# Scores of an attention kernel in four column tiles of 32 keys, with side pieces moved ahead of the branches

## The chip, the cores and the metric

The kernel runs on one core of a Trainium2 chip. The metric is the device time of one execution in microseconds (us); a measurement of this kernel tells changes of about 0.3% from no change.

## The reference, cut to what matters

Four blocks follow one another on x of shape (4, 2048, 256), each on the layernorm of x and added to x: attention A, a feed-forward block, attention B, the feed-forward block again. All weights are 256 x 256, and each attention has 16 heads of 16 channels.

```python
# attention A                                     # attention B
q, k, v = heads(xn @ Wq.T), ...                   k = decayed sums of heads(xn @ Wk.T), normed, scaled
scores = q @ k.T * 0.25, causal                   v = mix of v and v one later, normed, scaled
out = softmax(scores) @ v @ Wo.T                  y1 = softmax(k[1:] @ k.T, causal) @ v; out = y1 @ Wc.T
# feed-forward
x_prev = x one token earlier;  xr, xk = mixes of x and x_prev
out = sigmoid(xr @ Wr.T) * ((relu(xk @ Wk.T) ** 2) @ Wv.T)
```

## The kernel before, in words

**Instances and slots.** There are eight attentions (four batches, A and B), in the order of ATT (L48). Each is worked through in four instances of four heads (HG), so n runs from 0 to 31. head_group() (L52) cuts an instance into 68 groups: for each chunk of 512 queries (qc) and each block of 128 keys (kb) up to the diagonal, two groups of two heads, and at the diagonal narrower ones (512, 384, 256 and 128 queries wide). A group fills two PSUM banks with scores, keys on the 128 partitions and queries along the bank. The time of the program is written out by hand in slots, one slot per group: in slot s TensorE computes the scores of group s + 3 (scores, L998), then the products of the values with the probabilities of group s, where a set is due (products, L1034), and then the side pieces. ScalarE takes the exponential of one group, 128 x 1024 (L810), into probs. GpSimd zeroes the upper triangle in groups on the diagonal (L713), five of them per chunk.

**Scores.** One matmul (L1013) has 99 rows (the channels of q and k as split into bf16 parts, and three rows for a maximum), 128 keys as its weights and up to 512 queries as its moving operand, in bf16. It uses all 128 columns of the array. **Products.** One set is four matmuls in fp32, one per head (L1055), each with 17 weight columns written to PSUM partitions 32 j to 32 j + 16: four column tiles of 32. The trace counts every fp32 matmul twice, once for each pass, so a set of four shows as x8. Of the 68 slots, 36 have products.

**Side pieces.** Between these run the projections, layernorms and feed-forward blocks of other chunks, as jobs (job_list, L124): P projects a chunk for an attention A, MA finishes a chunk after attention A and prepares it for attention B, MB finishes it after attention B. Tables T_P, T_M and T_B (L112 to L118) give each piece a slot behind the job's t0. o0 and o1 (project_tokens, L870, matmul L875) are the output projection, t0, t1, bt0 and bt1 are transposes (turn, L857, matmul L860) that wait for the layernorm of VectorE (L1121 to L1130), u0 to u3 are projections of keys and queries (project_channels, L863, matmul L866). Side pieces use the whole array. P has 10 pieces with TensorE, MB 10 and MA 18. A job that belongs to an instance has its t0 three slots ahead of that instance's first slot, those of attention A of batch 1 have it 8 slots behind.

**Branches.** Where a head's scores could be too large for an exponential without a maximum, a flag is set. TensorE reads a flag per instance (L1083) and branches (L1084): into a body that first computes the maxima (maxima, L982; row_maxima, L962) and then 68 slots with a mask matmul (L1017) on the diagonal, or past it into the else part, 68 slots without. The branch of instance n stands in front of slot 68 n - 3. The two bodies lie behind each other in the instruction stream, so an instance without a flag jumps over the first body, and one with a flag jumps over the second when it is done. With these inputs four instances have a flagged head, one head each: n = 11, 15, 27 and 31, the last of each attention B. maxima() first waits for all the loads of keys and queries of the instance, which SyncE issues (load_keys, load_queries), then for each head reads a flag and branches again (L991).

**Order.** Each engine walks the slots in order. VectorE, ScalarE and GpSimd issue the jobs' steps in slots of the same tables. Score groups have three buffers (NS_BUF), so the scores of group g wait for the exponential of group g - 3, and probs has six.

Of the kernel before, what the change touches and what calls it, by code (L numbers as in the profile page):

```python
# [12 lines left out]
P = 128  # L13
# [4 lines left out]
CH = 512  # L18
NCH = S // CH
# [61 lines left out]
AHEAD = NS_BUF  # L81

FIRST_OF = [min(i for i, g in enumerate(GROUPS) if g[0][0][0] == qc) for qc in range(NCH)]
LAST_OF = [max(i for i, g in enumerate(GROUPS) if g[0][0][0] == qc) for qc in range(NCH)]
# [39 lines left out]
def job_list():  # L124
    def start(k, c):
        return (k * NHG + c) * NG

    jobs = [Job("P", 0, c, 0, -80 + 14 * c) for c in range(NCH)]
    for c in range(NCH):
        jobs.append(Job("P", 1, c, 1, start(0, c) + 8))  # L130
    for k, b in ((1, 0), (2, 1), (5, 2), (6, 3)):
        jobs += [Job("MA", b, c, k + 1, start(k, c) - 3) for c in range(NCH)]
    for k, b in ((3, 0), (4, 1)):
        for c in range(NCH):
            jobs.append(Job("MB", b, c, k, start(k, c) - 3))
            jobs.append(Job("P", b + 2, c, k + 1, start(k, c) + 29))
    jobs += [Job("MB", 2, c, 7, start(7, c) - 3 if c < 3 else start(7, 2) + 32) for c in range(NCH)]

    jobs += [Job("MB", 3, c, 7, start(7, 3) + (16, 37, 58, 82)[c]) for c in range(NCH)]
    jobs.sort(key=lambda j: j.t0)  # L140
    return jobs


JOBS = job_list()
FIRST_SLOT = -100
W_FIRST = (WQ, WK, WV)
# [96 lines left out]
def hybrid_kernel(nc, t, out):  # L243
    with ExitStack() as ctx:
# [571 lines left out]
        def _(pe):  # L816
# [27 lines left out]
            def setup(slot):  # L844
# [3 lines left out]
                if slot == JOBS[3].t0:  # L848
                    params()

            def free_bank(part):
                if part.before:
# [109 lines left out]
            def row_maxima(n, j):  # L962
                i0 = (n * HG + j) * NMP
                kk, qq = k_st[0:KROWS, j, :], q_st[0:KROWS, j, :]
                for i, (qb, b0, nb) in enumerate(MAX_PIECES):
                    if i >= MAX_BUF:
                        pe.wait_ge(s_mx["used"], i0 + i + 1 - MAX_BUF)
# [14 lines left out]
            def maxima(n):  # L982
                if n:
                    pe.wait_ge(s_probs, n * NG)
                for c in range(NCH):
                    pe.wait_ge(s_q[c], 16 * (len(Q_RUNS) + 1) * (n + 1))
                    pe.wait_ge(s_k[c], 16 * len(K_RUNS) * (n + 1))
                k, hg = divmod(n, NHG)
# [9 lines left out]
            def scores(g, masked):  # L998
# [10 lines left out]
                for bank, units in enumerate(GROUPS[i]):  # L1009
                    o = ps[:, 2 * (g % NS_BUF) + bank, :]  # L1010
                    for qc, kb, j, q0, w, col in units:
                        mask = masked and kb >= TB * qc
                        last = pe.matmul(o[:, col:col + w], k_st[0:KROWS, j, kb * P:(kb + 1) * P],  # L1013
                                         q_st[0:KROWS, j, qc * CH + q0:qc * CH + q0 + w], start=True, stop=not mask,
                                         skip_group_check=mask)
                        if mask:
                            last = pe.matmul(o[:, col:col + P], mask_qk[:, :], ident_b[:, :], start=False, stop=True,  # L1017
                                             skip_group_check=True)
                last.then_inc(s_scores, 1)
# [55 lines left out]
            for n in range(NI):  # L1075
# [7 lines left out]
                any_flag = pe.value_load(flags_of(k)[:, H + hg:H + hg + 1])  # L1083
                with pe.If(any_flag > 0):  # L1084
                    maxima(n)
                    slots(n * NG - AHEAD, (n + 1) * NG - AHEAD, True)
                with pe.Else():
                    pe.sem_inc(s_mx["scores"], NMP * HG)
                    pe.sem_inc(s_mx["turned"], HG)
                    slots(n * NG - AHEAD, (n + 1) * NG - AHEAD, False)  # L1090
            slots(NTOT - AHEAD, LAST_SLOT, False)

# [351 lines left out]
```

## Time and profile before

| | us |
|---|---|
| median of three runs | 3423.64 (3422.43 to 3432.76) |
| profiled execution, its own time | 3428.78 |
| span of the profiled execution | 3427.0 |
| mean granted clock of TensorE, share of full | 0.957 |
| busy: TensorE / ScalarE / VectorE / GpSimd | 3151.7 / 2291.9 / 1423.6 / 850.3 |

A row of the timeline view has the start in us, the us from start to end of what it merges, the engine, the line, the operation, out<-in, shapes and a count; in brackets stands the idle time before it and what ended it. A matmul's recorded length holds a tail of about 0.16 us in which the next one already runs, so the distance of two starts is the time that a matmul takes from the next. PEld is the weight load. "issue" means that the profile shows nothing that was waited for.

### The profile page before, as it was taken

To read this page: it belongs to the slowest core of one execution; us is meant where nothing else is said; L and a number is where in the kernel's file an instruction comes from. 1 tells how busy PE (TensorE), PEld (TensorE's weight loads), DVE (VectorE), ACT (ScalarE), POOL (GpSimd) and SP (SyncE) were. 2 spreads that over 40 slices of the span, in tenths; PEclk is the share of its full clock that TensorE was granted. 3 is DMA by queue.
4 is the path that set the end of the run, shared out by engine and by line. 5 is a ranking of instruction groups with operands and counts; after the bars stand their busy time and mean duration, and the time that the engine had idled before them with its cause. 6 is when DMAs were issued, how large, how long until landed. Compare 5 with 4: busy or idle time off the path is not lost.

```text
span 3427.0 us, 51952 instructions
## 1 busy us (share of the span) xinstructions
PE 3151.7 (92%) x19172; PEld 1212.5 (35%) x19172; DVE 1423.6 (42%) x3534; ACT 2291.9 (67%) x2487; POOL 850.3 (25%) x1278
## 2 busy tenths in 40 slices
PE   7999999999999789997999999999999989899897
PEld 4222233333333333332333333333333333333334
DVE  5222235545454542434233333445445545422434
ACT  2788767777676467674667676776777764688462
POOL 4111123333222222221222221323233221322111
PEclk9999999999999899998999999999999998999899
DMA  5222212222221123222212222121222211222111
GB/s 139 78 74 67 83 43 68 68 66 67 57 65 48 53 59 85 63 59 62 79 55 71 74 79 86 54 59 52 69 64 67 71 52 37 62 63 75 41 44 44
DMA packets 229682, 223.05 MB, mean 65 GB/s; under 512 B 33221, under 2 KB 212933, under 8 KB 229320
## 3 DMA queue, kind: packets, MB, share of 16 engines
q1 hardware_dynamic: 228504, 217.47, 22.2%
q8 instruction: 223, 3.65, 0.5%
q14 instruction: 139, 1.14, 0.1%
q10 hardware_dynamic: 816, 0.79, 0.1%
HBM read 146.80 MB, written 71.32 MB: 64 GB/s over the span
## 4 chain that ended last, share of the span: by engine, by line
PE 77%; DVE 10%; issue 7%; ACT 4%; POOL 1%; SPq 1%; DMA 1%; ACTq 0%; DVEq 0%; POOLq 0%
PE ps L1055 26%; PE ps L1013 25%; PE ps L875 12%; PE ps L866 10%; ACT probs L810 4%; DVE pmax L1349 2%; PE ps L860 2%; DVE ln_st L1121 1%; DVE xn L1130 1%; DVE o_blk L1391 1%; POOL v_st L691 1%; DVE x_buf L1242 1%; PE ps L903 0%; DVE nw_u L1111 0%; DVE nw_u L1113 0%
## 5 line engine op out<-in xcount | busy, mean ns | idle before, releaser
L810 ACT ACTIVATE probs<-ps 128x1024 f32<-128x1024 f32 x2176 | 2136.5, 1023 | 749.8 <-PE ps L1013 555.8
L1013 PE MATMUL ps<-q_st,k_st 99*128 99x512 bf16 (+3 forms) x5120 | 1204.3, 353 | 120.6 <-issue 103.5
L1055 PE MATMUL ps<-probs,v_st 128*17 128x512 f32 (+3 forms) x10240 | 1163.1, 535 | 41.9 <-ACT probs L810 16.2
L713 POOL TENSOR_SCALAR_AFFINE_SELECT probs<-probs 128x256 f32<-128x256 f32 (+1 forms) x896 | 423.4, 487 | 1705.9 <-ACT probs L810 1700.4
L1013 PEld LDWEIGHTS ps<-q_st,k_st 99*128 99x128 bf16 x5120 | 424.0, 98 | 1062.4 <-ACT probs L810 467.8
L1055 PEld LDWEIGHTS ps<-probs,v_st 128*17 128x17 f32 x10240 | 185.0, 96 | 534.5 <-issue 355.6
L1391 DVE STREAM_TRANSPOSE o_blk<-ps 128x512 f32<-128x512 f32 x128 | 90.8, 710 | 449.4 <-PE ps L1055 449.4
L866 PE MATMUL ps<-xT,wT 128*128 128x512 f32 x512 | 255.6, 625 | 1.6 <-issue 1.0
L1242 DVE TENSOR_TENSOR x_buf<-x_buf,ps 128x512 f32<-128x512 f32 x64 | 43.4, 679 | 380.1 <-PE ps L875 380.1
L637 POOL TENSOR_TENSOR parts<-rest,parts 128x512 bf16<-128x512 f32 x96 | 119.9, 1249 | 260.8 <-DVE parts L1153 260.8
L1266 DVE SCALAR_TENSOR_TENSOR buf_v<-buf_v,ps 128x512 f32<-128x512 f32 x64 | 44.0, 687 | 304.8 <-PE ps L875 304.8
L875 PE MATMUL ps<-wT,o_in 128*128 128x256 f32 x512 | 160.4, 468 | 1.0 <-issue 1.0
L662 POOL TENSOR_TENSOR buf_a<-xf 128x512 f32<-128x512 f32 x64 | 79.4, 1242 | 270.7 <-DVE xf L1136 255.2
L866 PEld LDWEIGHTS ps<-xT,wT 128*128 128x128 f32 x512 | 90.7, 193 | 140.9 <-issue 128.8
L866 PE MATMUL ps<-buf_k,wT 128*128 128x512 f32 x256 | 125.8, 616 | 8.3 <-DVE buf_k L1253 8.3
L875 PEld LDWEIGHTS ps<-wT,o_in 128*128 128x128 f32 x512 | 117.7, 236 | 41.5 <-issue 20.0
L875 PE MATMUL ps<-wT,buf_a 128*128 128x256 f32 x512 | 126.6, 391 | 0.5 <-issue 0.5
L875 PE MATMUL ps<-wT,buf_u 128*128 128x256 f32 x512 | 121.2, 380 | 2.2 <-issue 2.2
L760 ACT CAST parts<-ps 128x512 bf16<-128x512 f32 x64 | 37.4, 585 | 114.0 <-PE ps L866 114.0
L860 PE MATMUL ps<-ident,xn 128*128 128x128 f32 x512 | 83.7, 288 | 29.9 <-DVE xn L1130 14.5
L875 PEld LDWEIGHTS ps<-wT,buf_a 128*128 128x128 f32 x512 | 92.5, 190 | 48.7 <-issue 38.4
L972 PE MATMUL ps<-k_st,q_st 99*128 99x512 bf16 (+3 forms) x160 | 65.5, 525 | 45.9 <-issue 38.3
(136 smaller groups left out, 2152.0 us busy)
## 6 DMA issues: line engine op xcount, KB each, us to landing
part_a<-parts SPq DMA_DIRECT2D x192, 128.0 KB
x_buf<-in_L_attn_a_X SPq DMA_DIRECT2D x32, 512.0 KB, 4.5
q_st<-part_a SPq DMA_DIRECT2D x128, 128.0 KB
o_chan<-o_out SPq DMA_DIRECT2D x64, 256.0 KB, 2.4
o_in<-o_chan SPq DMA_DIRECT2D x64, 256.0 KB, 4.5
q_st<-part_b SPq DMA_DIRECT2D x128, 128.0 KB
k_st<-part_a SPq DMA_DIRECT2D x64, 192.0 KB, 2.9
part_b<-parts SPq DMA_DIRECT2D x96, 128.0 KB
```

The costliest lines, as they stand in the source:

```text
L637: pool.tensor_tensor(parts[:, u % NPARTS, 2, :], rest[:, u % 2, :], parts[:, u % NPARTS, 1, :], ALU.subtract).then_inc(s_low, 1)
L662: pool.tensor_tensor(buf_a[:, kt, :], xf[:, kt, 1:CH + 1], xf[:, kt, 0:CH], ALU.subtract).then_inc(s_diff, 1)
L713: last = pool.affine_select(out=o, in_=o, compare_op=ALU.is_ge, fill=0.0, base=0, pattern=[[0, o.shape[1]], [1, P]], channel_multiplier=-1)
L810: nc.scalar.activation(probs[:, g % NP_BUF, :], ps[:, bk:bk + 2, :].rearrange("p a n -> p (a n)"), ACT.Exp, scale=SCALE[ATT[g // (NHG * NG ...
L860: last = pe.transpose(ps[:, part.bank, tb * P:(tb + 1) * P], src[:, tb, kt * P:(kt + 1) * P], ident[:, :])
L866: last = pe.matmul(ps[:, part.bank, :], wT[:, w, kt, m * P:(m + 1) * P], src[:, kt, :], start=(kt == 0), stop=(kt == KT - 1))
L875: last = pe.matmul(ps[:, part.bank, i * D:(i + 1) * D], src[:, kt, tb * P:(tb + 1) * P], wT[:, w, kt, :], start=(kt == 0), stop=(kt == KT ...
L1013: last = pe.matmul(o[:, col:col + w], k_st[0:KROWS, j, kb * P:(kb + 1) * P], q_st[0:KROWS, j, qc * CH + q0:qc * CH + q0 + w], start=True, ...
L1055: last = pe.matmul(ps[32 * j:32 * j + VW, bank, q0:q0 + w], v_st[:, k % 2, kb, hg * HG + j, :], p, start=(kb == 0), stop=(kb >= TB * qc), ...
L1242: nc.vector.tensor_tensor(half(x, i), half(x, i), ps[:, part.bank, :], ALU.add).then_inc(s_side[part.bank], 1)
L1349: nc.vector.tensor_reduce(pmax[:, 1 if b0 else 0, qb:qb + 1], src, AX_X, ALU.max).then_inc(s_mx["used"], 1)
L1391: nc.vector.transpose(o_blk[:, sg % 2, :], ps[:, 6 + sg % 2, :]).then_inc(s_o, 1)
```

## The change

Every matmul of scores(), the one on keys and queries and the one that adds the mask, is issued as four, one for each 32 keys, each to 32 PSUM partitions, with the same moving operand. The jobs of an instance start one slot earlier (FRONT is -4), so that their first piece, o0, is issued in the last slot ahead of the branch; the P jobs of batch 1 start 27 slots earlier, so that u2 falls there; the lead-in starts 10 slots earlier. The branch tests for a flag of 0, and the body without maxima comes first. maxima() no longer waits for all loads; row_maxima waits for a chunk's loads ahead of the first block of queries of that chunk.

```diff
--- before.py
+++ after.py
@@ -80,6 +80,8 @@
 NP_BUF = 6
 AHEAD = NS_BUF
 
+FRONT = -AHEAD - 1
+
 FIRST_OF = [min(i for i, g in enumerate(GROUPS) if g[0][0][0] == qc) for qc in range(NCH)]
 LAST_OF = [max(i for i, g in enumerate(GROUPS) if g[0][0][0] == qc) for qc in range(NCH)]
 DIAG_OF = [min(i for i, g in enumerate(GROUPS) if g[0][0][0] == qc and g[0][0][1] == TB * qc) for qc in range(NCH)]
@@ -125,16 +127,16 @@
     def start(k, c):
         return (k * NHG + c) * NG
 
-    jobs = [Job("P", 0, c, 0, -80 + 14 * c) for c in range(NCH)]
+    jobs = [Job("P", 0, c, 0, -90 + 14 * c) for c in range(NCH)]
     for c in range(NCH):
-        jobs.append(Job("P", 1, c, 1, start(0, c) + 8))
+        jobs.append(Job("P", 1, c, 1, start(0, c) + FRONT - T_P["u2"]))
     for k, b in ((1, 0), (2, 1), (5, 2), (6, 3)):
-        jobs += [Job("MA", b, c, k + 1, start(k, c) - 3) for c in range(NCH)]
+        jobs += [Job("MA", b, c, k + 1, start(k, c) + FRONT) for c in range(NCH)]
     for k, b in ((3, 0), (4, 1)):
         for c in range(NCH):
-            jobs.append(Job("MB", b, c, k, start(k, c) - 3))
+            jobs.append(Job("MB", b, c, k, start(k, c) + FRONT))
             jobs.append(Job("P", b + 2, c, k + 1, start(k, c) + 29))
-    jobs += [Job("MB", 2, c, 7, start(7, c) - 3 if c < 3 else start(7, 2) + 32) for c in range(NCH)]
+    jobs += [Job("MB", 2, c, 7, start(7, c) + FRONT if c < 3 else start(7, 2) + 32) for c in range(NCH)]
 
     jobs += [Job("MB", 3, c, 7, start(7, 3) + (16, 37, 58, 82)[c]) for c in range(NCH)]
     jobs.sort(key=lambda j: j.t0)
@@ -142,7 +144,7 @@
 
 
 JOBS = job_list()
-FIRST_SLOT = -100
+FIRST_SLOT = -110
 W_FIRST = (WQ, WK, WV)
 W_LATER = (FR, FK, FV, BK, BV, WO, BC)
 LAST_SLOT = NTOT + 140
@@ -848,6 +850,12 @@
                 if slot == JOBS[3].t0:
                     params()
 
+            def matmul(o, kt, q, **how):
+
+                for c in range(0, P, 32):
+                    last = pe.matmul(o[c:c + 32], kt[:, c:c + 32], q, **how)
+                return last
+
             def free_bank(part):
                 if part.before:
                     pe.wait_ge(s_side[part.bank], part.before)
@@ -963,6 +971,9 @@
                 i0 = (n * HG + j) * NMP
                 kk, qq = k_st[0:KROWS, j, :], q_st[0:KROWS, j, :]
                 for i, (qb, b0, nb) in enumerate(MAX_PIECES):
+                    if qb % TB == 0:
+                        pe.wait_ge(s_q[qb // TB], 16 * (len(Q_RUNS) + 1) * (n + 1))
+                        pe.wait_ge(s_k[qb // TB], 16 * len(K_RUNS) * (n + 1))
                     if i >= MAX_BUF:
                         pe.wait_ge(s_mx["used"], i0 + i + 1 - MAX_BUF)
                     for bk in range(b0, b0 + nb):
@@ -982,9 +993,6 @@
             def maxima(n):
                 if n:
                     pe.wait_ge(s_probs, n * NG)
-                for c in range(NCH):
-                    pe.wait_ge(s_q[c], 16 * (len(Q_RUNS) + 1) * (n + 1))
-                    pe.wait_ge(s_k[c], 16 * len(K_RUNS) * (n + 1))
                 k, hg = divmod(n, NHG)
                 for j in range(HG):
                     flag = pe.value_load(flags_of(k)[:, hg * HG + j:hg * HG + j + 1])
@@ -1010,12 +1018,12 @@
                     o = ps[:, 2 * (g % NS_BUF) + bank, :]
                     for qc, kb, j, q0, w, col in units:
                         mask = masked and kb >= TB * qc
-                        last = pe.matmul(o[:, col:col + w], k_st[0:KROWS, j, kb * P:(kb + 1) * P],
-                                         q_st[0:KROWS, j, qc * CH + q0:qc * CH + q0 + w], start=True, stop=not mask,
-                                         skip_group_check=mask)
+                        last = matmul(o[:, col:col + w], k_st[0:KROWS, j, kb * P:(kb + 1) * P],
+                                      q_st[0:KROWS, j, qc * CH + q0:qc * CH + q0 + w], start=True, stop=not mask,
+                                      skip_group_check=mask)
                         if mask:
-                            last = pe.matmul(o[:, col:col + P], mask_qk[:, :], ident_b[:, :], start=False, stop=True,
-                                             skip_group_check=True)
+                            last = matmul(o[:, col:col + P], mask_qk[:, :], ident_b[:, :], start=False, stop=True,
+                                          skip_group_check=True)
                 last.then_inc(s_scores, 1)
 
             def values_there(n, qc):
@@ -1081,13 +1089,13 @@
                     for bk in SIDE_BANKS[:2]:
                         pe.wait_ge(s_side[bk], parts_before(bk, 0))
                 any_flag = pe.value_load(flags_of(k)[:, H + hg:H + hg + 1])
-                with pe.If(any_flag > 0):
-                    maxima(n)
-                    slots(n * NG - AHEAD, (n + 1) * NG - AHEAD, True)
-                with pe.Else():
+                with pe.If(any_flag == 0):
                     pe.sem_inc(s_mx["scores"], NMP * HG)
                     pe.sem_inc(s_mx["turned"], HG)
                     slots(n * NG - AHEAD, (n + 1) * NG - AHEAD, False)
+                with pe.Else():
+                    maxima(n)
+                    slots(n * NG - AHEAD, (n + 1) * NG - AHEAD, True)
             slots(NTOT - AHEAD, LAST_SLOT, False)
 
         @block.vector
```

## Rows read from the trace of the kernel before

**Rows 1.** The page: span, and busy time of each engine with its share.

```profile
span 3427.0 us, 51952 instructions
...
PE 3151.7 (92%) x19172; PEld 1212.5 (35%) x19172; DVE 1423.6 (42%) x3534; ACT 2291.9 (67%) x2487; POOL 850.3 (25%) x1278
```

**Rows 2.** The page's costliest groups: scores, and two sorts of token projections.

```profile
L1013 PE MATMUL ps<-q_st,k_st 99*128 99x512 bf16 (+3 forms) x5120 | 1204.3, 353 | 120.6 <-issue 103.5
...
L875 PE MATMUL ps<-wT,o_in 128*128 128x256 f32 x512 | 160.4, 468 | 1.0 <-issue 1.0
...
L875 PE MATMUL ps<-wT,buf_u 128*128 128x256 f32 x512 | 121.2, 380 | 2.2 <-issue 2.2
```

**Rows 3.** Timeline of TensorE, 578 to 589 us, within an instance.

```profile
578.56 0.61 PE L1013 MATMUL ps<-q_st,k_st 99*128 99x512 bf16 x2
579.00 1.89 PE L875 MATMUL ps<-wT,buf_u 128*128 128x256 f32 x8
580.73 0.60 PE L1013 MATMUL ps<-q_st,k_st 99*128 99x512 bf16 x2
581.26 1.05 PE L1055 MATMUL ps<-probs,v_st 128*17 128x512 f32 x8
...
583.21 1.05 PE L1055 MATMUL ps<-probs,v_st 128*17 128x512 f32 x8
...
588.10 0.66 PE L860 MATMUL ps<-ident,xn 128*128 128x128 f32 x4
```

**Rows 4.** Timeline of TensorE, 531 to 543 us, around a branch without a flag.

```profile
531.20 1.05 PE L1055 MATMUL ps<-probs,v_st 128*17 128x512 f32 x8 [1.41 <-POOL probs L713]
535.77 1.01 PE L1013 MATMUL ps<-q_st,k_st 99*128 99x512 bf16 x2 [3.52 <-issue]
536.58 3.48 PE L875 MATMUL ps<-wT,o_in 128*128 128x256 f32 x8
...
541.96 0.63 PE L1055 MATMUL ps<-probs,v_st 128*17 128x256 f32 x8
542.52 2.00 PE L875 MATMUL ps<-wT,o_in 128*128 128x256 f32 x8
```

**Rows 5.** Line 1084, the branch in TensorE's sequencer: min/median/max in ns.

```profile
L1084 PEldq COMPARE_BRANCH  x36: 82/3690/4694, 90.8 to 3371.7; - x36
```

**Rows 6.** Waits of TensorE: us in total, times, longest us.

```profile
PE ps L1013 <- issue: 103.5, 28, 7.7
...
PE ps L1055 <- POOL probs L713: 11.7, 14, 1.4
```

**Rows 7.** Window 533 to 540 us: busy per engine; PEclk is the granted clock.

```profile
533.00:540.00 7.00, 4.23 (x11) 3.04 (x12) 0.32 (x1) 1.02 (x1) 3.81 (x6) 0.51 0.42 111
```

**Rows 8.** Timeline of TensorE: first matmul of flagged instance 11, first after it.

```profile
1135.24 0.28 PE L972 MATMUL ps<-k_st,q_st 99*128 99x128 bf16 x1 [9.91 <-issue]
...
1266.36 1.01 PE L1013 MATMUL ps<-q_st,k_st 99*128 99x512 bf16 x2 [7.73 <-issue]
```

**Rows 9.** Groups by shape: scores 128 queries wide.

```profile
L1013 PE MATMUL ps<-q_st,k_st 99*128 99x128 bf16 x512 | 112.5, 220 | 0.0
```

**Rows 10.** Timeline of TensorE in a flagged instance: narrow scores and their mask.

```profile
1254.92 0.22 PE L1013 MATMUL ps<-q_st,k_st 99*128 99x128 bf16 x1
1254.98 0.22 PE L1017 MATMUL ps<-ident_b,mask_qk 128*128 128x128 bf16 x1
```

**Rows 11.** Timeline after the last branch: a run of narrow products, and its weight loads.

```profile
3375.55 1.49 PE L1055 MATMUL ps<-probs,v_st 128*17 128x384 f32 x24 [1.90 <-issue]
...
3376.21 0.34 PEld L1055 LDWEIGHTS ps<-probs,v_st 128*17 128x17 f32 x12 [0.20 <-issue]
```

**Rows 12.** Timeline of VectorE, 582 to 589 us: the last step of a layernorm.

```profile
586.63 1.38 DVE L1130 TENSOR_SCALAR xn<-x_buf,ln_mv,nw_y 128x256 f32<-128x256 f32 x4
```

**Rows 13.** Timeline of TensorE: first scores of the program.

```profile
94.99 4.43 PE L1013 MATMUL ps<-q_st,k_st 99*128 99x512 bf16 x16 [5.88 <-issue]
```

**Rows 14.** Timeline of ScalarE, 1002 to 1006 us: two exponentials in a row.

```profile
1004.36 1.94 ACT L810 ACTIVATE probs<-ps 128x1024 f32<-128x1024 f32 x2 [0.44 <-PE ps L1013]
```

## The prediction, made before the changed kernel ran

> **What bounds the kernel now.** I read the page's head first: TensorE is busy for 92% of the span and ScalarE for 67% [rows 1], so time is saved where TensorE stands between matmuls, or runs slowly. The costliest groups come next: 5,120 score matmuls [rows 2], 160 for each of 32 instances. Then the timeline inside an instance [rows 3]. Two scores behind side work take 0.44 us up to the next side piece (578.56 to 579.00), so 0.22 each. The same two take 0.53 up to the values' products (580.73 to 581.26). So going from the whole array to column tiles costs 0.09. A set of products 256 wide takes 0.56 up to the next matmul [rows 4]; one 512 wide, up to the scores, 0.98 (583.21 less four scores and 0.09 before it is 582.24, which is 0.98 behind 581.26). The extra 256 columns cost 0.42, so 512 are 0.85 and the way back costs 0.13. A pair of slots takes 1.95 (581.26 to 583.21), of which 0.22 goes into two switches: 0.11 each.
>
> The second loss is at the branches. Behind the products at 531.20 TensorE idles 3.52 us, with nothing waited for [rows 4]; the branch has a median of 3,690 ns [rows 5]. There are 28 such idle times, 103.5 us in all [rows 6]: 24 between two instances without a flag, 3 behind flagged ones (two jumps in a row, 7.73 us [rows 8]) and one at the start. The granted clock is 0.51 over 533 to 540 us, so most of that stretch is at 1.2 GHz, behind the idle time [rows 7]. The piece o0 issued there takes 3.48 us where its like takes 1.89 [rows 3, 4].
>
> **The change, part by part.** The sum is made against the profiled execution's 3,428.8 us, span 3,427.0; the median of 3,423.6 is 5 us below it.
>
> *Scores in tiles.* Now each of 36 product slots in an instance has a switch before it and one behind, 2,298 in all with those at the ends taken off. Afterwards scores and products share a mode, and only side pieces switch. By the tables they occupy 548 slots behind the first, each with a switch in and one out: 1,095. Some of these are new, where a side piece sits in a slot without products. 1,203 switches fewer at 0.11: **-132**. Against it stands the layernorm. xn is ready at 588.01 [rows 12] and the transposes start at 588.10 [rows 3] with no idle time: TensorE arrives just then. The seven slots before it become 0.7 us shorter, and VectorE's chain does not, so the 16 second layernorms of the MA jobs give that back: **+12**. The first layernorm of each job already keeps TensorE waiting, partly for the taking of a segment queued behind it, and t0 moves to a slot ahead of that dependence, so I charge nothing there; if that cover fails it is another +20.
>
> Does a group of four take 0.22 as the one matmul did? The products show four tiles side by side, but in fp32. The trace has no bf16 ones. The densest stretch has 24 matmuls in 1.49 us, and within it 12 weight loads in 0.34, three groups of four about 0.12 apart [rows 11]. So 0.22 for a group is within what the queue has fed, and I take 0 extra. The upper bound is the mean of the same stretch, 0.062 per load and matmul: 0.25 a group, +0.03 x 5,120 = +154. Below, nothing is gained, as the moving operand is as long as before. Scores 128 wide are another matter: today the matmul behind one starts 0.06 later [rows 10], and the densest groups of four are about 0.11 apart. There are 512 [rows 9], so 0 to +26, plus the masks of four instances; I take a middle value of 0.03, **+15**.
> The Trainium skill has a rule against this part: in "TensorEngine Tiling (Array Packing)", Restrictions and Gotchas, column tiling switches Fast Weight Load off. With "TensorE: Matmul & The Clock Gate", LDWEIGHTS, a load takes its columns over 1.2 GHz, 107 ns for four times 32; by this estimate the 512 narrow groups would cost 24 us in place of 15, the wide ones nothing. No run so far shows it for bf16.
>
> *A piece ahead of the branch.* The sequencer passes on o0's eight matmuls before it jumps, so they run in the fetch's shadow. At full clock they take 1.73 (579.00 to 580.73, [rows 3]). 24 boundaries x 1.73: **-42**. u2 in front of the first instances is as long. The idle time left is 3.5 - 1.7 = 1.8 us. o0 and o1 are 160.4 us busy, the equally long L875 group on buf_u 121.2 [rows 2]; of the 39 us between them some 10 belong to the flagged instances, and the scores beside them (1.01 against 0.60 us [rows 3, 4]) add about 5. If 1.8 us of idle time no longer brings the clock down, that is **-34**; bounds 0 and -45.
>
> *The branch turned round.* Between two unflagged instances nothing changes: a taken jump at the entry becomes one at the exit, both at the same place. Behind a flagged one both jumps go, at three places: 7.73 + 1.6 each, **-28**. At the end of instance 31 its exit jump goes as well: 1.90 [rows 11], **-2**. At the start 3.7 us of jump go [rows 5, 13], but TensorE's queue is now passed by P of batch 1, chunk 0: its layernorm (up to 7.1 us, from 580.9 to 588.0 [rows 3, 12]) can start only behind the flags, then come two transposes and u0 to u2. Instance 0 starts some 8 us later and has 6 us less in it: **+2**. VectorE, SyncE (its loads) and GpSimd are passed by the same job, and wait for nothing that isn't there by then. In front of each of the four flagged instances there are now two jumps. Today's 9.91 us of idle time [rows 8] is loads that are still coming, then four inner flags. Two jumps take as long as those loads or longer, less the cover of o0. From -2.6 to +6.8 each; I take 1.5, as the longest jump is 4.7 [rows 5]: **+6**.
>
> *Waits by chunk.* Behind two jumps all loads are there: **0**. Without the jumps it would be worth some part of the 9.91 us at each of four places. Only TensorE's own maxima are queued behind these waits, and VectorE, which takes them.
>
> *One slot earlier.* GpSimd's values for the next attention (L691) now come ahead of the first diagonal mask of the last chunk, not between two. The 11.7 us that products wait for masks [rows 6] go: **-12**, at worst 0. The DMAs of the jobs start a slot earlier on SyncE's queue, ahead of the branch's place, and their data is needed a slot earlier too: 0.
>
> Sum: -132 + 12 + 15 - 42 - 34 - 28 - 2 + 2 + 6 + 0 - 12 = **-215**. 3,428.8 - 215 = 3,213.8, and 5 less for the median: **3,209**.
>
> **The rivals.**
>
> *ScalarE sets the pace.* Two exponentials in a row take 1.94 - 1.02 = 0.92 from start to start [rows 14], 1.84 a pair, while TensorE would do 1.74. Then a pair without side work gains 0.11, not 0.21. For it: in such stretches ScalarE is already nearly always busy. Against it: TensorE gains 0.05 to 0.07 a slot on it and may be some two slots ahead, so it takes about 27 slots without side work to catch up, and every side piece of 1.7 us resets that. If it bound in half the pairs, some 50 us would be lost: 3,259. Chance 0.12.
>
> *The clock still falls.* Idle time of 1.8 us still brings 1.2 GHz, and the fetch under load is longer than the cover. Then the 34 go, and half of the 42 may: 3,209 + 34 + 21 = 3,264, up to 3,290. Chance 0.10.
>
> *The feed of instructions binds.* Scores go from 5,120 loads and matmuls to 20,480. If a pair of them takes 0.062 us, as the mean in rows 11 has it, a group takes 0.25: 3,209 + 154 = 3,363. For it: no longer stretch of the trace is that dense. Against it: 12 loads in 0.34 us in the same stretch, and products between the scores need only half the rate. Chance 0.10.
> The Trainium skill, "TensorE: Matmul & The Clock Gate", says that the sequencer's microcode spends about 62 ns for a MATMUL when hardware decoding is off; four are 0.248 us, which gives about the same time. The 12 loads speak neither for nor against it, since it counts matmuls.
>
> *Slower than before: tiles in bf16 do not run side by side.* The same moving operand is then read four times in turn, wholly or in part. Four in a row would take 0.88 and add 0.66 x 5,120 = 3,380: 6,600 us. With half an overlap, 0.44 a group, +1,126: 4,335. It decides from 215 / 5,120 = 0.042 us on, a group of 0.262. For it: a bf16 operand of 512 columns passes in 0.22 and an fp32 one in twice 0.42, so the rate of columns per tile would be twice what the products have shown. Against it: at two passes and four bytes the products move the same bytes per us and tile. Chance 0.07.
>
> **How the numbers follow.** The forecast has 0.58, the rivals 0.12, 0.10, 0.10 and 0.07, and 0.03 lies between the last two, within 0.3% of before. The median is predicted by the likeliest, 3,209. Its own bounds (masks not gained, narrow scores at +26, the first layernorm at +20 on one side; 34 to 45 for the clock and shorter idle time on the other) give 3,160 to 3,260. With the first two rivals the range is 3,150 to 3,295; what is left out is the feed, the serial tiles and the case between, 0.20. Faster by over 0.3% (about what a measurement can tell): 0.58 + 0.12 + 0.10 + 0.10 = 0.90; within it 0.03; slower 0.07.
>
> **What would show it.** Right: pairs of slots start 1.74 to 1.78 us apart; no 0.11 between scores and products; four score matmuls start within 0.03 of one another and groups 0.22 apart. At the boundaries o0 stands in front of 1 to 2 us of idle time, in windows where the clock stays at full; flagged instances have over 9 us before L972 and none behind them. The layernorm before bt0 shows TensorE waiting for VectorE. Wrong: groups of scores over 0.24 apart would mean feed or port; a pair at 1.84 with ScalarE back to back means ScalarE; a clock of half behind each boundary takes the 34 away; and a new wait for xn at t0 as well would cost up to 20.

## The result, and the profile after

| | before | after |
|---|---|---|
| median | 3427.38 us (3422.43 to 3432.76, 6 runs) | 3447.16 us (3445.12 to 3456.79, 6 runs) |
| span of the profiled execution | 3427.0 | 3443.4 |
| mean granted clock | 0.957 | 0.942 |

The ratio is 1.0062, 95% interval 1.005 to 1.0073: 20 us slower, where 215 us less had been forecast. The forecast was wrong in sign, and its range, 3,150 to 3,295, missed by 152 us. The page's head, beside [rows 1]:

```profile
span 3443.4 us, 84234 instructions
...
PE 3067.8 (89%) x35300; PEld 1346.3 (39%) x35300; DVE 1444.8 (42%) x3534; ACT 2241.7 (65%) x2487; POOL 833.8 (24%) x1278
```

TensorE is busy 84 us less and the span is 16 longer: what the tiles won came back as idle time. In the densest stretch the tiles do what was forecast. TensorE's timeline:

```profile
520.24 1.04 PE L856 MATMUL ps<-q_st,k_st 99*32 99x512 bf16 x16
521.10 1.03 PE L1063 MATMUL ps<-probs,v_st 128*17 128x512 f32 x8
521.96 1.04 PE L856 MATMUL ps<-q_st,k_st 99*32 99x512 bf16 x16
...
637.71 1.05 PE L856 MATMUL ps<-q_st,k_st 99*32 99x384 bf16 x32
638.58 1.03 PE L1063 MATMUL ps<-probs,v_st 128*17 128x512 f32 x8
```

A pair of slots starts 1.72 us behind the last (1.95 before, [rows 3]). Four groups of four score matmuls take 0.86, so 0.215 a group, and the switch to the products is gone. At 637.71 eight groups, two 384 wide, two 128 and four 256, take 0.87 us, no more than their 2,048 columns do at 0.215 for 512: narrow groups cost nothing extra. The waits of TensorE (us in total, times, longest), before, beside [rows 6], and after:

```profile
PE ps L860 <- DVE xn L1130: 14.5, 2, 9.6
...
PE ps L860 <- DVE o_blk L1391: 11.1, 29, 0.6
PE ps L1055 <- issue: 10.1, 26, 1.9
```

```profile
PE ps L1063 <- issue: 63.4, 56, 2.6
PE ps L856 <- issue: 57.9, 29, 3.7
PE ps L868 <- DVE o_blk L1399: 57.8, 29, 2.4
PE ps L868 <- DVE xn L1138: 51.3, 19, 13.8
PE ps L983 <- issue: 50.5, 5, 13.5
PE ps L1063 <- ACT probs L812: 25.3, 17, 2.0
```

A segment is what the products of one chunk of queries sum up in one bank, and VectorE takes it out with the transpose into o_blk. The idle time in front of scores with nothing waited for (L856) has fallen from 103.5 to 57.9, and L983, the first matmul of a flagged instance, has risen from 38.3 to 50.5. Both moved the way that was forecast; the rise of 12 is twice the 6 forecast. New are the transposes t0 (L868), which wait 57.8 us for the taking of a segment where it was 11.1, and 51.3 for xn where it was 14.5, and the products (L1063), where 63.4 was 10.1. By the trace's records of the granted clock, 399 us now run at 1.2 GHz (48 stretches) where it was 294 (36). In instance 6, TensorE before, from o1 to t0, and after:

```profile
640.80 1.99 PE L875 MATMUL ps<-wT,o_in 128*128 128x256 f32 x8
...
650.44 0.63 PE L860 MATMUL ps<-ident,xn 128*128 128x128 f32 x4 [0.34 <-DVE o_blk L1391]
```

```profile
628.10 1.99 PE L883 MATMUL ps<-wT,o_in 128*128 128x256 f32 x8
631.79 1.05 PE L856 MATMUL ps<-q_st,k_st 99*32 99x512 bf16 x16 [1.70 <-issue]
...
634.90 1.99 PE L883 MATMUL ps<-wT,o_in 128*128 128x256 f32 x8
...
637.27 0.61 PE L1063 MATMUL ps<-probs,v_st 128*17 128x256 f32 x8
...
642.07 0.61 PE L856 MATMUL ps<-q_st,k_st 99*32 99x512 bf16 x8
644.83 0.81 PE L868 MATMUL ps<-ident,xn 128*128 128x128 f32 x4 [2.15 <-DVE o_blk L1399]
645.57 1.04 PE L856 MATMUL ps<-q_st,k_st 99*32 99x512 bf16 x8
648.64 1.91 PE L1063 MATMUL ps<-probs,v_st 128*17 128x512 f32 x8 [2.03 <-ACT probs L812]
```

And VectorE after, in the same stretch:

```profile
637.01 0.69 DVE L1250 TENSOR_TENSOR x_buf<-x_buf,ps 128x512 f32<-128x512 f32 x1 [4.33 <-PE ps L883]
637.81 1.41 DVE L1129 BATCH_NORM_STATS2 ln_st<-x_buf 128x6 f32<-128x256 f32 x4
...
642.68 1.38 DVE L1138 TENSOR_SCALAR xn<-x_buf,ln_mv,nw_y 128x256 f32<-128x256 f32 x4
643.98 0.71 DVE L1399 STREAM_TRANSPOSE o_blk<-ps 128x512 f32<-128x512 f32 x1
...
646.31 0.67 DVE L1399 STREAM_TRANSPOSE o_blk<-ps 128x512 f32<-128x512 f32 x1
...
647.86 0.68 DVE L1144 COPY xf<-ps 128x512 f32<-128x512 f32 x1
```

o0 (628.10) does cover the branch: 1.70 us of idle time, at full clock. But o1 (634.90) now stands ahead of the instance's last products (637.27), and VectorE issues the layernorm (637.81 to 644.06) ahead of the taking of those products (643.98). TensorE is at t0 at 642.68 and waits 2.15 us, where instance 6 waited 0.34 before. xn is ready at 644.06; what t0 waits for last is the taking of that last segment (643.98 to 644.69), since t0's bank is the one that it lay in. Then the products at 648.64 wait again. The view names ScalarE, whose probs had long been there; what ended then is VectorE's copy of t0 (647.86 to 648.54). t0 is now in slot 5, and seg_at gives that slot bank 7, which these first products of chunk 1 are to fill. In slot 6, before, it was bank 6. In the instances on either side this second stall is put down to "issue" (2.5 to 2.6 us), which is most of the new 63.4; run e14 below, with t0 in the other bank, has 7.5 there. The window that holds both stalls:

```profile
644.00:653.00 9.00, 6.14 (x44) 2.18 (x48) 4.99 (x13) 2.20 (x4) 1.04 (x1) 0.62 0.42 118
```

TensorE is busy 6.14 of 9 us, and the clock is mostly at the lower level (0.62): 1.2 GHz from 645.1 to 652.0, from just behind the first of the two waits. At the start of the program, in TensorE's, SyncE's and VectorE's timelines:

```profile
102.58 1.97 PE L868 MATMUL ps<-ident,xn 128*128 128x128 f32 x8 [13.79 <-DVE xn L1138]
...
115.42 1.30 PE L856 MATMUL ps<-q_st,k_st 99*32 99x512 bf16 x16 [2.74 <-issue]
```
```profile
84.40 5.59 SPq L435 DMA_DIRECT2D part_a<-parts  x9
90.03 1.11 SPq L421 DMA_DIRECT2D x_buf<-in_L_attn_a_X  x1
```
```profile
96.91 1.41 DVE L1129 BATCH_NORM_STATS2 ln_st<-x_buf 128x6 f32<-128x256 f32 x4 [7.64 <-DMA x_buf<-in_L_attn_a_X]
```

The moved job's load of x stands behind nine stores on SyncE's queue. Its layernorm starts at 96.91, and the first scores come 20.4 us later than before (94.99, [rows 13]).

### The profile page after: what moved, and what is told of

Read it like the earlier page. It is cut to its first block, busy times and chain, and to the rows that moved or that the text cites. A ratio compares the mean times of both kernels' runs of the same rounds, so it can differ in the third digit from the quotient of the medians.

```text
span 3443.4 us, 84234 instructions
## 1 busy us (share of the span) xinstructions
PE 3067.8 (89%) x35300; PEld 1346.3 (39%) x35300; DVE 1444.8 (42%) x3534; ACT 2241.7 (65%) x2487; POOL 833.8 (24%) x1278
## 3 DMA queue, kind: packets, MB, share of 16 engines
q8 instruction: 345, 5.65, 0.7%
## 4 chain that ended last, share of the span: by engine, by line
PE 74%; DVE 13%; issue 7%; ACT 3%; SPq 1%; DMA 1%; POOL 0%; DVEq 0%; ACTq 0%; POOLq 0%
PE ps L856 24%; PE ps L1063 24%; PE ps L883 12%; PE ps L874 11%; ACT probs L812 3%; PE ps L868 3%; DVE pmax L1357 2%; DVE ln_st L1129 2%; DVE xn L1138 2%; DVE nw_u L1119 1%; DVE nw_y L1123 1%; DVE nw_u L1121 1%; DVE x_buf L1250 1%; DVE ln_mv L1132 1%; DVE o_blk L1399 1%
## 5 line engine op out<-in xcount | busy, mean ns | idle before, releaser
L812 ACT ACTIVATE probs<-ps 128x1024 f32<-128x1024 f32 x2176 | 2076.7, 1082 | 787.3 <-PE ps L856 783.5
L856 PE MATMUL ps<-q_st,k_st 99*32 99x512 bf16 (+3 forms) x20480 | 1264.9, 354 | 75.9 <-issue 57.9
L1063 PE MATMUL ps<-probs,v_st 128*17 128x512 f32 (+3 forms) x10240 | 1197.5, 544 | 92.3 <-issue 63.4
L856 PEld LDWEIGHTS ps<-q_st,k_st 99*32 99x32 bf16 x20480 | 496.1, 96 | 965.6 <-issue 584.4
L715 POOL TENSOR_SCALAR_AFFINE_SELECT probs<-probs 128x256 f32<-128x256 f32 (+1 forms) x896 | 408.5, 472 | 1639.4 <-ACT probs L812 1617.9
L1063 PEld LDWEIGHTS ps<-probs,v_st 128*17 128x17 f32 x10240 | 273.8, 99 | 387.8 <-issue 151.4
L868 PE MATMUL ps<-ident,xn 128*128 128x128 f32 x512 | 98.1, 325 | 113.4 <-DVE o_blk L1399 57.8
L868 PEld LDWEIGHTS ps<-ident,xn 128*128 128x128 f32 x512 | 64.8, 162 | 182.0 <-DVE xn L1138 135.0
L883 PE MATMUL ps<-wT,o_in 128*128 128x256 f32 x512 | 131.6, 401 | 0.2 <-issue 0.2
L983 PE MATMUL ps<-k_st,q_st 99*128 99x512 bf16 (+3 forms) x160 | 66.7, 533 | 57.0 <-issue 50.5
L883 PEld LDWEIGHTS ps<-wT,buf_u 128*128 128x128 f32 x512 | 92.3, 189 | 62.0 <-issue 51.8
```

The source lines that it names most:

```text
L715: last = pool.affine_select(out=o, in_=o, compare_op=ALU.is_ge, fill=0.0, base=0, pattern=[[0, o.shape[1]], [1, P]], channel_multiplier=-1)
L812: nc.scalar.activation(probs[:, g % NP_BUF, :], ps[:, bk:bk + 2, :].rearrange("p a n -> p (a n)"), ACT.Exp, scale=SCALE[ATT[g // (NHG * NG ...
L856: last = pe.matmul(o[c:c + 32], kt[:, c:c + 32], q, **how)
L868: last = pe.transpose(ps[:, part.bank, tb * P:(tb + 1) * P], src[:, tb, kt * P:(kt + 1) * P], ident[:, :])
L883: last = pe.matmul(ps[:, part.bank, i * D:(i + 1) * D], src[:, kt, tb * P:(tb + 1) * P], wT[:, w, kt, :], start=(kt == 0), stop=(kt == KT ...
L1063: last = pe.matmul(ps[32 * j:32 * j + VW, bank, q0:q0 + w], v_st[:, k % 2, kb, hg * HG + j, :], p, start=(kb == 0), stop=(kb >= TB * qc), ...
```

## The experiments

Sixteen kernels, each compared with the kernel before on the same chip. Names in quotes are pieces of the tables. Differences between runs are differences of ratios times 3,426; by the intervals each is known to 6 to 12 us either way. Waits are those of one profiled execution of each run.

**e1: the tiles alone.**

```diff
-  last = pe.matmul(o[:, col:col + w], ...)        # scores and mask
+  last = matmul(o[:, col:col + w], ...)           # four of 32 keys
```


> The kernel before, with the scores in four column tiles and nothing else. Theory A (the jobs' shift by one slot is what costs: it puts t0 into the slot ahead of products that need its bank, and the layernorm ahead of the taking of the last segment): the tiles alone keep nearly what was forecast for them, 120 us less some layernorm waits, so 3,290 to 3,335 us. Theory B (TensorE's gain anywhere comes back as waits for VectorE's chains, with or without the shift): 3,395 to 3,430 us, with waits before the transposes about as long as in the changed kernel.


Measured 3379.97, ratio 0.9869 (0.9852 to 0.9885), between the ranges of the two theories: 45 us, not the 105 forecast, though not none either. In the waits:

```profile
PE ps L854 <- issue: 119.9, 29, 8.3
...
PE ps L866 <- DVE o_blk L1397: 31.4, 29, 1.4
PE ps L1061 <- POOL probs L713: 24.2, 18, 2.2
PE ps L866 <- DVE xn L1136: 23.6, 18, 9.6
```

These four have grown by 16, 20, 12 and 9 us, and half-clock time by 54, which costs 27. Every engine that TensorE hands work to keeps its pace, and shorter slots leave it less time.

**e2: tiles, branch and chunk waits, and only o0 a slot earlier.**

```diff
-T_M = {"load": -10, "o0": 0, "o1": 2, "t0": 9, ...
+T_M = {"load": -10, "o0": -1, "o1": 2, "t0": 9, ...
```


> The changed kernel, but of each job of an instance only the piece o0 is one slot earlier (offset -1, the job's start back at -3), and the P jobs of batch 1 and the lead-in are where they were. Theory A: no idle time of 2 us before t0 nor behind it, the clock stays up there, o0 still covers a good half of the jump: 3,200 to 3,270 us. Theory B: waits come back elsewhere, 3,330 us or more.


Measured 3293.47, ratio 0.9614 (0.9586 to 0.9641), again between the ranges, and much nearer to theory A's. **e3: the change with P and the lead-in as before**, and **e4: before, with the shifts of the jobs and nothing else**:

```diff
# e3                                       # e4
-start(0, c) + FRONT - T_P["u2"]           -start(k, c) - 3
+start(0, c) + 8                           +start(k, c) + FRONT     (and P, lead-in)
```


> The changed kernel, with the P jobs of batch 1 and the lead-in where they were before; the other jobs are still one slot earlier. The lead-in of the changed kernel is 24.6 us longer than before, and instances 0 to 3 together are 22.8 shorter. Both theories: the stalls at t0 stay. If the 27-slot shift is a loss, 3,425 to 3,440 us; if it pays for itself, 3,447 or more.

> The kernel before, with the jobs' shift alone (one slot for an instance's jobs, 27 for P of batch 1, lead-in 10), scores in whole matmuls, branch and maxima as before. Theory A: the bank and the order of VectorE's steps are wrong here too, so although o0 covers the jump the time goes up: 3,460 to 3,540 us, with idle time before and behind t0 and a clock of half there. Theory B: slots are as long as before, so no chain is late and o0's cover shows: 3,370 to 3,400 us.


e3: 3432.2, ratio 1.0014 (1.0 to 1.0027). e4: 3547.1, ratio 1.036 (1.0342 to 1.0377), a little above its range. Between e2 and e3 stand only the other pieces of MA and MB jobs, a slot earlier each: 0.0400, 137 us. P's shift is the rest, 0.0048 or 16 us. e4 has neither the tiles nor the turned branch and loses 123 us all the same, with o0 ahead of its branches: the shift needs neither of them to cost time.

**e5 and e6: e2 with one more piece a slot earlier.**

```diff
# e5                       # e6
-"o1": 2                   -"t0": 9
+"o1": 1                   +"t0": 8
```


> e2_o0_alone with o1 one slot earlier as well, in slot -2 of its instance, and t0 left where it is (slot 6). VectorE then issues the layernorm of 6 us ahead of the taking of the last segment of the instance before (slot -1). If this order is half of what the jobs' shift costs: 3,320 to 3,385 us, against 3,293 of e2_o0_alone, with the first products of the second chunk waiting. If the order is harmless, since taking has slack, the layernorm is one slot earlier and the time is 3,280 to 3,300 us.

> e2_o0_alone with t0 alone one slot earlier, in slot 5, so that its part lies in the bank that the products of slot 6 fill next; o1 stays. If the bank is what costs: products of slot 6 wait for VectorE's copy behind t0, two us in each of 28 instances and a clock of half behind it, 3,345 to 3,430 us. If only the layernorm's lateness counts, one slot of waiting more before t0, 0.9 us each: 3,310 to 3,325 us.


e5: 3345.64, ratio 0.9751 (0.9729 to 0.9774), 47 us over e2. e6: 3385.81, ratio 0.9882 (0.9859 to 0.9904), 92 over e2. Both lie in the range of the theory that the move costs. Added up they are the 137 us, so the other 15 pieces of an MA job cost nothing that shows. e5's waits have a new row, and e6's have xn up from 28.4 and ScalarE up from 15.0:

```profile
PE ps L1061 <- DVE o_blk L1397: 42.7, 26, 1.7
```
```profile
PE ps L866 <- DVE xn L1136: 75.4, 47, 9.7
...
PE ps L1061 <- ACT probs L810: 35.1, 24, 1.8
PE ps L1061 <- issue: 23.3, 42, 1.0
```

**e12: e6 with t0's part in the other bank. e13: e5 with the layernorm issued behind the taking. e14: e3 with both.**

```diff
# e12 (seg_at)                       # e13 (m_job of VectorE), e14 with + 3
-if i > FIRST_OF[qc]                 +yield j.t0 + 2
+if i + (qc == 1) > FIRST_OF[qc]      for i in range(2): dve.wait_ge(...)
                                      layernorm(j)
```


> Run e6 (t0 a slot earlier, 3,386 us) with one thing changed: the side piece in slot 5 of an instance goes to the bank that chunk 0's products have just left, not to the one that chunk 1's are about to fill. If the bank is what made t0's slot dear: TensorE's wait of products for ACT probs falls from 35 us to about e2's 15 and the time to 3,340 to 3,365 us. If it is only the earlier need of the layernorm (75 us of waiting for xn): 3,375 to 3,395 us, with the wait for xn unchanged.

> Run e5 (o1 a slot earlier, 3,346 us) with one thing changed: VectorE issues the first layernorm of MA and MB jobs one slot behind o1, so it stands behind the taking of the last products of the instance before, as it does in the kernel before. If the 52 us of e5 over e2 come from that order (the taking queued behind 6.3 us of layernorm, and the products of the next instance behind the taking): 3,290 to 3,310 us. If they come from the earlier o1 itself (its wait for o_in, its place between products): 3,335 to 3,350 us.

> Run e3 (the change without the shift of P and of the lead-in, 3,432 us) with the layernorm behind the taking, as in run e13, and the side piece in slot 5 in the other bank, as in e12. If order and bank are what the shift of the jobs costs, and t0's earlier need the rest: 3,432 less 52 less 25 is 3,355 us, 3,340 to 3,370 us. If the layernorm, now starting in the old slot with t0 a slot earlier, gives it back as waiting for xn: 3,385 to 3,430 us.


e12: 3361.03, ratio 0.9802 (0.9778 to 0.9826), 27 us better than e6; ScalarE's row is at 15.0 again and L1061's issue at 5.6, so both of e6's rows were waits for the bank, though the view names others. The 27 us are the least that bank 7 costs, since the other bank has a price too. There t0 needs the taking of chunk 0's segment, as in e2: it waits 67.6 us for the taking and 28.9 for xn in e12, 32.1 and 28.4 in e2, 2.5 and 75.4 in e6. The other 64 us are what t0 costs one slot earlier with the bank and the waits of e2: VectorE's layernorm and taking end no sooner for it. e13: 3334.05, ratio 0.9724 (0.9707 to 0.9741). My theory fell: the order is worth some 9 us of 47, no more than such a difference is known to. The products' wait of 42.7 is gone, and t0 waits in its place (25.7 in e5):

```profile
PE ps L866 <- DVE o_blk L1398: 63.8, 29, 2.7
```

e14: 3401.17, ratio 0.9921 (0.9902 to 0.994), 32 better than e3, about the 27 + 9 of the two repairs; the other 105 us of the shift stay. It lies in the second range, but not as said there: t0's wait for xn hardly rose (45.1 us, e3 42.6), its wait for the taking did (98.7, e3 57.8).

**e8: e2 with more room for the layernorms. e10: tiles alone with it. e15, e16: e8 with o1 a slot earlier, e16 also with the layernorm behind the taking.**

```diff
-"t0": 9, "t1": 11, "diff": 11, "shift": 13 ... "bt0": 34, "bt1": 36 ... "vb": 64
+"t0": 10, "t1": 12, "diff": 12, "shift": 14 ... "bt0": 35, "bt1": 37 ... "vb": 63
```


> e2_o0_alone with the transposes one slot later (t0 and t1 at 10 and 12, bt0 and bt1 at 35 and 37, with what follows the former) and GpSimd's values for the next attention one slot earlier (63). If TensorE's gain comes back only where a chain was cut to fit, this frees most of the 32 us that it waits for o_blk, part of the 28 for xn and 20 of the 24 for masks: 3,220 to 3,265 us. If VectorE's chain as a whole is the bound: 3,285 to 3,300 us, with waits at the next pieces instead.

> Only the tiles (run e1, 3,380 us), with t0, t1, diff and shift one slot later, bt0 and bt1 one slot later and vb one slot earlier. If the gain that is missing in e1 is mostly VectorE's layernorms, which don't get shorter with the slots, this gives back what e8 did over e2, 32 us, or more: 3,335 to 3,352 us, with the waits for xn under 12 us. If it is mostly the clock behind the uncovered jumps, the waits go but the time doesn't: 3,362 to 3,380 us.

> Run e8 (t0 and bt0 a slot later, 3,262 us) with o1 a slot earlier, as e5 has it over e2 (52 us there). If those 52 us are time that the first layernorm lacks before t0, the later t0 takes most of it up: 3,262 to 3,280 us. If they are the products behind the branch, which wait 43 us in e5 for the taking that stands behind the layernorm, t0's slot changes nothing there: 3,295 to 3,315 us, with that wait above 35 us again.

> Run e15 with the layernorm behind the taking, as in e13. In e13 this took the products' wait away, but t0 waited 64 us instead of 26. With t0 a slot later there is room for it: if order and room together are the whole cost of the earlier o1, 3,262 to 3,278 us, no more than 16 over e8, and t0's wait for the taking under 40 us. If the earlier o1 costs something by itself (its place, the clock behind the longer idle time at the branch), 3,285 us or more.


e8: 3261.74, ratio 0.9517 (0.9499 to 0.9534), 33 us under e2 and the fastest of all; its waits for the taking, for xn and for masks are 33 us shorter than e2's in all (52.1 against 84.8). e10: 3346.77, ratio 0.9773 (0.9753 to 0.9792), 33 under e1, so the room is worth the same with or without o0. Which of its three parts (t0, bt0, vb) brings how much was not tried. e15: 3309.45, ratio 0.9661 (0.9639 to 0.9684), in its second range: the products' wait is 42.8 us again. e16: 3296.95, ratio 0.9622 (0.96 to 0.9645), 36 us over e8 with order and room both right, where I had set 16 as the most if these were the whole cost. What o1 costs by its place is seen in instance 6 of e8 and of e16, from the last products of the instance before to t0:

```profile
613.84 0.62 PE L1061 MATMUL ps<-probs,v_st 128*17 128x256 f32 x8
614.39 1.99 PE L881 MATMUL ps<-wT,o_in 128*128 128x256 f32 x8
...
624.29 0.63 PE L866 MATMUL ps<-ident,xn 128*128 128x128 f32 x4 [0.59 <-DVE o_blk L1397]
```
```profile
620.47 3.17 PE L881 MATMUL ps<-wT,o_in 128*128 128x256 f32 x8
...
624.02 0.61 PE L1061 MATMUL ps<-probs,v_st 128*17 128x256 f32 x8
...
633.54 0.63 PE L866 MATMUL ps<-ident,xn 128*128 128x128 f32 x4 [2.25 <-DVE o_blk L1398]
```

In e8 TensorE has o1 to do while VectorE takes those products, and is at t0 9.86 us behind them (624.29 - 0.59 - 613.84). In e16 it is there after 7.27 and waits. VectorE's way, taking, layernorm, taking, is only 0.9 us shorter (10.45 against 9.52). o1 was cover for VectorE. The longer idle time also brings the lower clock: e16 has 28 us more idle time than e8 and 30 more at 1.2 GHz, worth 15; the spans differ by 39.

**e7: branch and chunk waits alone. e9 and e11: e2 and e8 with branch and waits as before.**

```diff
-with pe.If(any_flag > 0):        # maxima(n), masked slots first
+with pe.If(any_flag == 0):       # slots without mask first
```


> The kernel before with the branch turned round and the maxima's waits by chunk, nothing else. By the prediction's terms: three pairs of jumps behind flagged instances go (28 us), the jump at the start (4) and at the end (2), four flagged instances have 1 to 3 us more before them: 3,395 to 3,410 us. If jumps are only moved and the sum stays: 3,420 to 3,430 us.

> The tiles and o0 ahead of the branch as in run e2, but the branch and the waits of maxima() as before. Theory one, the two jumps of a flagged instance only change places (from behind it to in front of it, as run e7 had it): 3,280 to 3,305 us, no different from e2's 3,293; behind each flagged instance a gap of 6 to 8 us, in front some 8 less than e2's. Theory two, the turned branch is worth what I forecast (28 less 6) once o0 covers the plain jumps: 3,310 to 3,325 us.

> Run e8 (3,262 us) with the branch and the waits of maxima() as before. If the turned branch only changes places of its jumps: 3,250 to 3,275 us. If it brings what was forecast (22 to 28 us): 3,280 to 3,295 us.


e7: 3429.51, ratio 1.0003 (0.9993 to 1.0014), nothing. e9: 3311.16, ratio 0.967 (0.9649 to 0.9691), 19 us over e2. e11: 3280.51, ratio 0.9572 (0.9552 to 0.9591), 19 over e8. So the turned branch is worth 19 us with o0 ahead of it, and nothing without: e9 and e11 lie in the range of the theory that it is worth something, e7 in that of jumps that only change places. In e7 the idle time in front of scores is 19.4 us shorter than before (84.1, 103.5 in [rows 6]) and that in front of flagged instances 18.7 longer (57.0, before 38.3). From e9 to e2 the former falls by 25.4 and the latter rises by 18.5, and 9.5 us of idle time before products go too. Why o0 makes that difference no run shows. The start of e7 gives back what it wins, since P's layernorm doesn't end earlier. Its first scores come 3.7 us sooner than before [rows 13], its first t0 no sooner; here before, then e7:

```profile
113.64 0.60 PE L860 MATMUL ps<-ident,xn 128*128 128x128 f32 x4
```

```profile
91.27 3.66 PE L1013 MATMUL ps<-q_st,k_st 99*128 99x512 bf16 x16 [2.35 <-issue]
...
113.90 0.66 PE L860 MATMUL ps<-ident,xn 128*128 128x128 f32 x4 [2.60 <-DVE xn L1130]
```

## Why the prediction was wrong

By ratios the parts add up to what was measured (e1, e9 less e1, e2 less e9, e3 less e2, after less e3):

| part | forecast | measured |
|---|---|---|
| tiles: switches, second layernorm, narrow scores | -132 + 12 + 15 = -105 | -45 |
| o0 ahead of the branch, and the clock | -42 - 34 = -76 | -68 |
| branch turned, chunk waits, ends | -28 - 2 + 2 + 6 = -22 | -19 |
| jobs a slot earlier | -12 | +137 |
| P and lead-in | 0 beyond the +2 above | +16 |
| sum | -215 | +21 |

**The step that failed** is the sentence on the first layernorm: "t0 moves to a slot ahead of that dependence, so I charge nothing there". I had looked at one dependence of t0, the taking of chunk 0's segment, and priced the loss of its cover at 20. The shift of the jobs cost 137 us. Three things were behind it. t0's slot decides its bank, and slot 5 has the bank that the next products fill (at least 27 us, e12). VectorE's chain in front of t0 ends no sooner for t0's being earlier (64 us, e12 over e2). And o1 was moved too, out of the stretch between VectorE's taking and t0, where it was the work that hid VectorE (47 us, e5, of which 36 are left with order and room put right, e16). With o1 moved, t0 isn't even ahead of the takings: it waits for that of the last segment, which o1's move has put behind the layernorm. I had priced every piece as time on TensorE, which a move doesn't change, and none as cover for another engine.

**One slot earlier** (masks, -12) was not tested by itself. In the profile after, the products wait 2.9 us for GpSimd, where it is 24.2 with the tiles alone, so this wait did go; whatever that is worth is in the +137.

**Tiles.** The switches went as computed, the pair of slots at 1.72 us even a little under the 1.74 forecast. The terms that were mis-sized are the ones against: narrow scores, +15, measured nothing; +12 for the layernorms measured 33, if the room that e10 gives to both layernorms and to the masks is counted (e1 to e10), and nothing was set down for more half-clock time. With room given, 78 of the 105 us are there (e10). Of the rest, the trace of e10 has 14 us more idle time at branches than before (117.5 against 103.5), 8 more in the wait for the taking (19.1 against 11.1) and 17 us more at half clock; that this is the cause was not tried.

**o0 and the clock** were right to 8 us: idle time behind o0 is 1.3 to 2.5 us in e2 (instances 1 to 3, which have no piece ahead there, and the flagged ones aside), where 1.8 was forecast, and most of those boundaries stay at full clock (e2 and e8 have 23 half-clock stretches, e1 has 41).

**The branch** was right in size, but only in company with o0, and in part by luck: the same edits without o0 bring nothing (e7), which the terms would not have said. The share of it at the start was wrong, both here and for **P**. "VectorE, SyncE (its loads) and GpSimd are passed by the same job, and wait for nothing that isn't there by then" looked at what they wait for, and not at what stands ahead on SyncE's queue: nine stores, 5.59 us together. The first branch comes at 114.2 us where e3 has it at 90.4, 23.8 later where some 8 were forecast for instance 0. The stores are 5.6 of that, and the load's data are there 6.9 us behind its issue (90.03 to 96.91), which the prediction didn't count; no run moved either. Instances 0 to 3 give 16 us back (319.9 against 335.9), since P is no longer in them. That leaves 8 in the profiled executions, and 16 by the ratios.

**The rivals.** The feed and the serial tiles did not come. The Trainium skill, "TensorE: Matmul & The Clock Gate", has about 62 ns for a MATMUL with hardware decoding off; at 637.71 it is 0.87 us for 32, 27 ns each, so that case doesn't hold here, and no run shows its price. By "TensorEngine Tiling (Array Packing)" column tiling switches Fast Weight Load off, from which I had estimated 24 us for narrow groups; the same row shows 0 within what can be read. No run here shows whether that mode was on. ScalarE as the pace did not show: pairs stay at 1.72 us, and exponentials still wait 783 us for scores in the profile after. The half clock did come, not behind the branches but behind the new waits. And slower than before came by a mechanism that I had given no chance: the rival on that side was the wrong one.

## What to carry to other kernels

Before a piece of work is moved, ask three things of it: what it needs and when that is ready by its own clock, which buffer or bank its new place gives it and who fills that next, and which other engine's work it hides where it stands now. On every engine that serves the piece, write down the order of issue behind the move, the DMA queue's too. When slots get shorter, give the hand-overs to slower engines a slot more in the same step: here that alone was worth 33 us, and e8, with that room and of all the shifts only o0's, takes 3261.74 us against 3428.22 and 3447.16.

## What the runs showed of the hardware that was not expected

- In the kernel after, the granted clock was at 1.2 GHz at each of the 27 places where t0 and the next products both wait, by 1.5 to 2.7 us with 1.8 us of work between; in instance 6 it fell just behind the first wait (645.1). One idle time of 3.5 at a branch has the lower clock too [rows 4, 7]. Single ones of 1.3 to 2.5 us behind o0 mostly do not: in e2 it came with 6 of 20. Where it does come it costs: in e16 o1 took 3.17 us, 2.3 behind such a gap of 1.89, and 1.99 in e8. So a small added wait can cost nearly twice its length: e13 has 24.5 us more idle time than e2, 44 more at half clock, and a span 47 longer.
- Column tiles in bf16 with 32 weight columns run side by side at the rate of one whole matmul (0.215 us for four of 512 columns), and groups of 384, 256 and 128 columns together take their share of that (0.87 for 2,048).
- With four times as many score matmuls the instruction DMA took 0.7% of the 16 engines' time, before 0.5% (5.65 MB, before 3.65).

```profile
q8 instruction: 345, 5.65, 0.7%
```
